# Copying a node table in interleaved 4 KB runs, and pacing GpSimd's gathers by small memsets

## What is computed

```python
deg = segment_sum(ones, row, num_segments=n)              # row = src, col = dst
deg_inv = where(deg > 0, rsqrt(maximum(deg, 1.0)), 0.0)
norm = deg_inv[row] * deg_inv[col]
h_j = h[col]                                              # h = relu(layernorm(x))
c_e = comps[edge_type]
msg = einsum('ebd,bdf->ef', c_e[:, :, None] * h_j[:, None, :], bases)
msg = msg * alpha[edge_type] * norm[:, None]
out = x + segment_sum(msg, row, num_segments=n)
```

## Time and profile before

| | us |
|---|---|
| median of 3 runs | 745.38 (742.51 to 745.63) |
| the profiled execution | 752.15 |
| its span | 750.2 |
| busy: DVE / PE / POOL / ACT | 596.4 / 574.7 / 540.3 / 370.1 |
| GpSimd's first scatter starts | 212.62 |
| its last scatter starts | 742.16 |

### The profile page before, as it was taken

How to read it: one execution, slowest core, us unless ns; L and a number is a source line. 1 busy time by engine, 2 the same in 40 slices (tenths; PEclk the granted TensorE clock), 3 DMA queues, 4 the chain that set the end, 5 groups by cost and what they waited for, 6 DMA issues and landing times.

```text
span 750.2 us, 13642 instructions
## 1 busy us (share of the span) xinstructions
PE 574.7 (77%) x3922; PEld 406.0 (54%) x3922; DVE 596.4 (80%) x2624; ACT 370.1 (49%) x1494; POOL 540.3 (72%) x404
## 2 busy tenths in 40 slices
PE   4999985665676876987778788886797878888860
PEld 4666654443454645655556565655565656665430
DVE  7999995466775676886987899986998999998730
ACT  0345542244424678664545655645656534446530
POOL 3788886455555587778788888878878767767775
PEclk9999998687788899999998999999999999999995
DMA  8999999989833335444535455444455545544332
GB/s 272 287 326 339 331 361 323 319 296 327 307 101 81 70 54 122 79 92 69 109 52 100 92 86 95 96 81 95 82 95 96 92 78 78 86 57 82 35 36 25
DMA packets 56574, 108.89 MB, mean 145 GB/s; under 512 B 9339, under 2 KB 48264, under 8 KB 55684
## 3 DMA queue, kind: packets, MB, share of 16 engines
q0 software_dynamic: 34496, 25.72, 25.6%
q1 hardware_dynamic: 4416, 50.68, 18.7%
q10 hardware_dynamic: 17588, 31.62, 13.5%
HBM read 94.89 MB, written 64.61 MB: 213 GB/s over the span
## 4 chain that ended last, share of the span: by engine, by line
DVE 14%; DMA 13%; issue 10%; PE 9%; POOL 8%; ACT 7%; ACTq 0%; POOLq 0%
DMA out_dram<-acc,scatter_idx 11%; POOL out_dram L393 6%; DVE masked L481 4%; DVE part_sum L518 4%; PE pst L756 3%; PE pst L737 3%; DVE turned_hot L475 2%; POOL rows L372 2%; DVE same L537 2%; ACT acc L651 2%; DMA rows<-in_x_dram,dst_i 2%; DVE rows L518 2%; ACT scratch L603 2%; PE pst L764 1%; ACT scratch L595 1%
## 5 line engine op out<-in xcount | busy, mean ns | idle before, releaser
L393 POOL DMA_INDIRECT out_dram<-acc,scatter_idx x196 | 313.8, 1601 | 106.3 <-issue 53.7
L372 POOL DMA_INDIRECT rows<-in_x_dram,dst_i x196 | 224.4, 1145 | 96.4 <-issue 36.2
L737 PE MATMUL pst<-table_bits,turned_hot 128*128 128x198 f16 x1568 | 183.1, 267 | 84.0 <-DVE masked L481 61.1
L756 PE MATMUL pst<-bases_sb,h_turned 128*128 128x512 f32 x392 | 214.1, 629 | 0.0
L737 PEld LDWEIGHTS pst<-table_bits,turned_hot 128*128 128x128 f16 x1568 | 147.3, 105 | 113.6 <-issue 59.1
L518 DVE SCALAR_TENSOR_TENSOR part_sum<-pst,coef,part_sum 128x128 f32<-128x128 f32 x392 | 115.7, 343 | 96.2 <-ACT part_sum L641 89.3
L764 PEld LDWEIGHTS pst<-rows,same 128*128 128x128 f32 x392 | 73.0, 199 | 166.2 <-issue 152.1
L641 ACT ACTIVATE part_sum<-pst,coef 128x128 f32<-128x128 f32 x196 | 71.2, 363 | 183.4 <-PE pst L756 132.3
L481 DVE SCALAR_TENSOR_TENSOR masked<-iota_h,lo,pst 128x198 f32<-128x198 f16 x392 | 141.9, 415 | 20.9 <-PE pst L737 16.3
L764 PE MATMUL pst<-rows,same 128*128 128x128 f32 x392 | 82.7, 294 | 58.4 <-ACT acc L651 57.4
L651 ACT ACTIVATE acc<-pst,sum_scale 128x128 f32<-128x128 f32 x196 | 71.5, 365 | 58.5 <-DMA out_dram<-acc,scatter_idx 28.9
(11 more groups left out here) (71 smaller groups left out, 415.8 us busy)
## 6 DMA issues: line engine op xcount, KB each, us to landing
out_dram<-in_x_dram SPq DMA_DIRECT2D x46, 1000.0 KB
src_row<-src_rows ACTq DMA_DIRECT2D x25, 512.0 KB
edge_row<-edge_rows ACTq DMA_DIRECT2D x45, 256.0 KB
out_dram<-in_x_dram ACTq DMA_DIRECT2D x4, 1000.0 KB
rows<-in_x_dram,dst_i POOLq DMA_INDIRECT x196
out_dram<-acc,scatter_idx POOLq DMA_INDIRECT x196
rows<-edge_rows ACTq DMA_DIRECT2D x10, 175.0 KB
edge_row<-edge_rows SPq DMA_DIRECT2D x4, 256.0 KB
```

Source lines behind the costliest of these rows:

```text
L372: pool.indirect_dma_start(row(t), None, x, bass.IndirectOffsetOnAxis(ap=dst_i[:, t:t + 1], axis=0)) \
L393: pool.indirect_dma_start(out, bass.IndirectOffsetOnAxis(ap=scatter_idx[:, t:t + 1], axis=0), acc[:, t % ACC_RING, :], None, compute_op=AL ...
L737: last = pe.matmul(pst[:, LOOK + t % 2, k * LO:(k + 1) * LO], turned_hot[:, g % 2, c, k * W + j * P:k * W + (j + 1) * P], table[:, c * LO: ...
L756: pe.matmul(pst[:, PRODUCT + t % 4, :], h_turned[:, g % 2, j, :], bases_sb[:].rearrange("d b f -> d (b f)"), start=True, stop=True).then_i ...
```

## The change

The first part replaces the copy's access pattern. Two consecutive transfers now share a block of 4,096 rows: one takes the even runs of 8 rows (4,096 bytes), the other the odd runs, 256 runs each. There are 48 such transfers of 1,048,576 bytes, and a 49th of the last 1,696 rows in the old form. The second part changes how gathers ahead of the copies' end are held back: 56 to 119 are each preceded by two memsets of a 128 by 40 tile, with a wait for the end of each, instead of waits on PE. `FIRST_GATHERS` rises from 108 to 120, and with it `gathers_until` and `stats_until`.

```diff
-    HIST_GATHERS = 56
-    LOOK_GATHERS = HIST_GATHERS + 4 * FIRST_LOOK * GROUP // 3
-    FIRST_GATHERS = LOOK_GATHERS + 3 * GROUP * SUM_STEP
+    HIST_GATHERS, FIRST_GATHERS = 56, 120
...
-    COPIES = 50
-    COPY_ROWS = N // COPIES
+    RUN_ROWS, RUNS = 8, 256
     COPY_RING = 2
+    PAIR_ROWS = 2 * RUNS * RUN_ROWS
+    COPIES = 2 * (N // PAIR_ROWS) + 1
+    LAST_COPY = (COPIES // 2) * PAIR_ROWS
...
+        beat = sb("beat", [P, 40])
...
-            a = i * COPY_ROWS
-            flat_out, flat_x = (y[a:a + COPY_ROWS, :].rearrange("r d -> (r d)") for y in (out, x))
-            engine.dma_start(flat_out.rearrange("(q e) -> q e", q=32), flat_x.rearrange("(q e) -> q e", q=32)) \
-                .then_inc(copied[i % COPY_RING], 16)
+            if i < COPIES - 1:
+                a = i // 2 * PAIR_ROWS
+                to, of = (y[a:a + PAIR_ROWS, :].rearrange("(q s r) d -> s q (r d)", s=2, r=RUN_ROWS)[i % 2]
+                          for y in (out, x))
+            else:
+                to, of = (y[LAST_COPY:N, :].rearrange("r d -> (r d)").rearrange("(q e) -> q e", q=32)
+                          for y in (out, x))
+            engine.dma_start(to, of).then_inc(copied[i % COPY_RING], 16)
...
-                elif HIST_GATHERS <= t < LOOK_GATHERS:
-                    pool.wait_ge(look_ps, (t - HIST_GATHERS) * FIRST_LOOK * GROUP // (LOOK_GATHERS - HIST_GATHERS) + 1)
-                elif LOOK_GATHERS <= t < FIRST_GATHERS:
-                    tile, part = divmod(t - LOOK_GATHERS, 3)
-                    if part == 0:
-                        pool.wait_ge(product_ready, tile + 1)
-                    else:
-                        pool.wait_ge(look_ps, FIRST_LOOK * GROUP + 2 * tile + part)
+                elif HIST_GATHERS <= t < FIRST_GATHERS:
+                    for _ in range(2):
+                        beats[0] += 1
+                        pool.memset(beat[:], 0.0).then_inc(beat_ended, 1)
+                        pool.wait_ge(beat_ended, beats[0])
```

More of the change, by code:

```diff
@@ L111, in sums_at @@
         return list(range(a + (b - a) * j // GROUP, a + (b - a) * (j + 1) // GROUP))
-    COPIES = 50
-    COPY_ROWS = N // COPIES
+    RUN_ROWS, RUNS = 8, 256
     COPY_RING = 2
+    PAIR_ROWS = 2 * RUNS * RUN_ROWS
+    COPIES = 2 * (N // PAIR_ROWS) + 1
+    LAST_COPY = (COPIES // 2) * PAIR_ROWS
     FIRST_COPIES = 4
-    assert COPIES * COPY_ROWS == N and COPIES % COPY_RING == 0
+    assert LAST_COPY < N and (N - LAST_COPY) * D % 32 == 0
     rows16_dram = nc.dram_tensor("edge_rows", (3, TILES * P), F16, kind="Internal").ap()
@@ L231, in build @@
         idx_ready = sem("idx_ready")
+        beat_ended = sem("beat_ended")
         type_row_loaded = [sem(f"type_row_loaded{b}") for b in range(TYPE_RING)]
@@ L301, in copy, with copies_done @@
                 engine.wait_ge(copied[i % COPY_RING], 16 * (i // COPY_RING))
-            a = i * COPY_ROWS
-            flat_out, flat_x = (y[a:a + COPY_ROWS, :].rearrange("r d -> (r d)") for y in (out, x))
-            engine.dma_start(flat_out.rearrange("(q e) -> q e", q=32), flat_x.rearrange("(q e) -> q e", q=32)) \
-                .then_inc(copied[i % COPY_RING], 16)
+            if i < COPIES - 1:
[6 more added lines that the diff above has]
+            engine.dma_start(to, of).then_inc(copied[i % COPY_RING], 16)
+        def copies_done(engine):
+            for b in range(COPY_RING):
+                engine.wait_ge(copied[b], 16 * len(range(b, COPIES, COPY_RING)))
         block = ctx.enter_context(nc.Block())
@@ L333, in _ @@
             sp.wait_ge(spare_filled, 16)
-            for b in range(COPY_RING):
-                sp.wait_ge(copied[b], 16 * (COPIES // COPY_RING))
+            copies_done(sp)
             for b in range(2):
@@ L351, in _ @@
                                pattern=[[1, P]], channel_multiplier=-1).then_inc(ident_ready, 1)
+            beats = [0]
             def pace(t):
@@ L381, in _ @@
             pool.wait_ge(spare_filled, 16)
-            for b in range(COPY_RING):
-                pool.wait_ge(copied[b], 16 * (COPIES // COPY_RING))
+            copies_done(pool)
             for t in range(TILES):
```

## The result

The changed kernel takes 772.75 us (median of 4 runs, 770.98 to 776.41), the kernel before 745.07 beside it (742.51 to 745.63). The ratio is 1.0385, with a 95% interval of 1.034 to 1.043. The forecast was 740 us, so it has the wrong sign. The profiled execution took 776.41 us with a span of 774.4; before it was 752.15 and 750.2. So 24.2 us have to be found in the two traces.

A forecast was written before the change was run, and what follows sets the result against it. GpSimd was taken to bound the kernel from 257 to 591 us. Terms -3.8 - 3.75 + 0 + 0 + 2 = -5.5 against the profiled 752.15 gave 746.6; with the median at 0.991 of profiled time, 740 us, range 728 to 757.

The forecast's parts named there:

- the price of a piece in part 2: DRAM copy: 4,096-byte pieces cost 175 to 215 ns, 0 to 31 us longer; 3 taken, end at 218 (215 to 246).
- 2.9 us for twelve gathers: Copy's end: the 12 added gathers cost 12 x 0.24 us of all sixteen DMA engines, so it ends 2.9 us later.
- rival A: Copy at the SBUF price: S, GpSimd's scatter start, at 246, 20 us late; +10, or 755 us; chance 0.21.
- Any S up to 226 is free: GpSimd's scatter start S: up to 226 us costs 0, because the eleventh scatter waits for `acc` until 254.63 anyway.
- given back as far as compute runs ahead: Behind the late scatter start: 8 of 19 idle us in 591 to 700 recovered, `acc` holding three tiles beyond today's lead.
- Part 1, the tail, -3.8: Main loop's end: twelve gathers moved ahead let 4.25 steps run at 10.64 instead of 11.54 us; -3.8, bounds 0 and -16.1.
- Part 2, the front, -3.75: Before the main loop: shorter copy pieces let an edge row load in time, removing DVE's 3.75 us wait; between 0 and 5.7.
- The Trainium skill's rule on packets: DMA queues: engines change queues only between packets, typically 9 to 17 descriptors; the front term would be 0 instead of -3.75.
- Part 3: Gathers ahead of the copy's end: two memsets make a 1.7 us cycle, the 64 gathers end at 217, ahead of 226; 0.
- wrong if the front changes by more than 6 us: Test set for the front: little there hangs on DMA but one wait, so a change above 6 us refutes the prediction.
- Rival C: Front gains 10 us rather than 3.75, as loads and instruction fetches no longer queue behind 64,000 bytes; -14, 731 us; chance 0.12.
- Part 4, +2: ACT's order: steps 8, 9 and 10 get one more 3.1 us statistics group each, partly hidden; +2, bounds 0 and 9.3.

The follow-up runs named there:

- e1: Kernel before with only the new copy (4,096-byte pieces, every second run), 108 gathers held back by the old waits: 773.6 us, ratio 1.0264 to the kernel before.
- e3: Changed kernel with its 4,096-byte pieces side by side, each transfer without gaps, the sixteen DMA engines on neighbouring pieces: 748.75 us, ratio 0.9939 to the kernel before.
- e12: Changed kernel with the old copy and six memsets instead of two ahead of each of 64 gathers, so that GpSimd starts late: 795.87 us (before 757.64).
- e2: Changed kernel with the old copy (64,000-byte pieces), keeping 120 gathers and the beat of two memsets: 748.56 us, ratio 0.994 to the kernel before.
- e17: Kernel before with the beat of two memsets alone, its own copy and 108 gathers: 742.8 us, ratio 0.9887 to the kernel before.
- e6: Changed kernel with interleaved copy runs of 32,768 bytes, every second one, instead of 4,096: 746.63 us, ratio 1.0047 to the kernel before.
- e8: Changed kernel with the old copy and 108 gathers instead of 120, beat kept: 743.79 us, ratio 1.0004 to the kernel before.
- e16: Kernel before with only the copy changed, to 8,192-byte runs side by side; own waits and 108 gathers: 751.42 us, ratio 0.9985 to the kernel before.
- e18: Changed kernel with 8,192-byte copy runs side by side and 108 gathers instead of 120, beat kept: 742.56 us, ratio 0.9874 to the kernel before.
- e11: Kernel before, unchanged, profiled once more: 750.31 us, where another single execution on the same chip took 757.64.
- e7: Changed kernel with the old copy, 120 gathers, and neither memsets nor waits ahead of the 57th to 120th: 748.7 us, ratio 1.0025 to the kernel before.

## Why the prediction was wrong, point by point

**The step that failed is the price of a piece in part 2.** The two ends, 175 and 215 ns for 4,096 bytes, were worked out, and then 3 of the 31 us between them were taken, because "a kilobyte is no dearer in small pieces" and the difference was put "down to the kind of transfer". The runs show 222 ns. Put into the same working: 12,288 x 47 / 16 = 36 us, 212.3 + 36 + 2.9 = 251.2; the copy ended at 250.9. So even the upper end, 246, was too low. That the sum meets the measured end to 0.3 us is in part luck: its 2.9 us for twelve gathers do not show, since e1 has 108 gathers and its first scatter comes at 252.42, no earlier. The reason was wrong in a second way. The prediction asked what the size of a piece costs, and on that it was nearly right: without gaps, e3 shows 184 ns and a start at 225.8. What it never asked is what the pattern of addresses costs. The 215 ns came from broadcast loads, which read one and the same run of DRAM for all 128 partitions, so that they stood near 222 is a coincidence, not a confirmation of rival A's reason.

**The free limit held.** "Any S up to 226 is free" gives 251 - 226 = 25 us; the eleventh scatter is 25.0 us late (279.65 against 254.63) and the thirteenth 24.95. e3, with its first scatter at 225.81, costs nothing.

**Rival A had the mechanism, at 755.** With S = 251 instead of 246 its own sum is 25 - 8 - 3.8 + 2 = +15, or 760 us. Another 12 are missing, 9 of them in the profiled execution. Its 8 us "given back as far as compute runs ahead" did not come, and e12 against the changed kernel shows the same: 19.4 us at the start are 19.6 at the end. The rows say where they went. Behind the last gather GpSimd did catch up, to 14.5 us late at tile 126, but the turned groups, which is compute, were then 24.1 us late and stayed so, with DVE busy for 55.08 of the 59 us from 591 to 650. So GpSimd had to wait for `acc` again, and the idle time in the earlier trace rows was no slack but the wait for that chain. That the ring of six `acc` is what had made compute as late as GpSimd is argued, not tested: 57.8 us of ACT's idle time ahead of the copies into `acc` are put down to scatters, 31.0 of them the one wait above.

**Part 1, the tail, -3.8: about -2, and not to be seen in time.** The four steps from the 31st to the 35th turned group took 38.7 us instead of 40.8, so the twelve gathers gave 2.1 us. GpSimd's lead at tile 126 was gone by tile 162, 23.6 us late again, and at the last scatter 1.3 us are left of what it had caught up since tile 108. The row of 10.2 us steps, given as the reason for a lower bound of 0, was the better guide than the mean of 11.54. Nor do the times show it: with the same old copy, 120 gathers had 0.994 (e2, before at 753.12) and 108 had 0.9887 (e17, before at 752.87), and on one chip 120 gathers took 746.63 us (e6, whose copy was no slower) and 108 took 743.79 (e8).

**Part 2, the front, -3.75.** In the trace it is there: from the first to the fifth turned group 65.8 us instead of 69.3, -3.5, and a load of an edge row lands in 10.3 us, with 2.2 us of DVE's idle left. In time it is not. e16, which has only that, is at 0.9985: its first to fifth turned group takes 66.9 us, but the first came later (141.18), so that the fifth is at 208.03, no earlier than before (205.84). And e18, whose fifth comes at 192.44 against 197.97 in e17, takes the same time as e17. The Trainium skill's rule on packets (DMA: Bandwidth & Descriptors, section "Queues, rings and completion order"), cited in the prediction, decides nothing here: SP's queue shows one packet for each 4,096-byte piece (4,938 for 19.00 MB, completions counted). The prediction left open how a copy in DRAM is packed, but the earlier trace rows has it: 777 packets for 24.64 MB are 385 pieces of 64,000 bytes and about as many completions, one packet a piece.

**The other front, which the prediction put at nothing.** Part 3 costed the beat (1.57 us in most cycles and 1.65 in the mean against 1.7, from 116.1 us on instead of 108.0, end at 221.4 against 217, both under 226) but never what the removed waits on PE's counters cost. The first turned group came 4.8 us earlier, and "wrong if the front changes by more than 6 us" came true: it is 8.3 us at the fifth. Rival C had the size but gave it to the DMA; e1, with the new copy and the old waits, has its fifth group at 207.5. In the changed kernel the copy hides all of it.

**Part 4, +2: nothing in the end, though larger on its way.** Two copies of turned groups on ACT (the 9th and the 13th) show it:

```profile
304.31 0.58 ACT L640 ACTIVATE h_turned<-pst 128x512 f32<-128x512 f32 x1
...
365.95 0.58 ACT L640 ACTIVATE h_turned<-pst 128x512 f32<-128x512 f32 x1
```

From the 9th to the 13th it takes 61.6 us, before 48.3 (283.39 to 331.73). By the 18th the lateness is back at 24.4. e2, which has the 120 gathers and their order of statistics, takes 61.4 us there, and e8, with 108, 48.2. So it comes with the order, and GpSimd hides it: its scatters stay 23 to 26 us late all through this stretch.

**Sum, as measured at GpSimd's scatters:** +24.95 us at the thirteenth, +0.65 from there to tile 108, -1.35 from there to the last: 24.25, against 24.2 in the spans.

## What to carry to other kernels

Price a DRAM-to-DRAM copy by its pattern of addresses as well as by the size of its pieces: here 4,096-byte pieces side by side were nearly free, the same pieces with gaps cost a fifth more on top, and one run of the pattern alone would have told it. When the unknown price of one edit sets when an engine that is already the bound may start, take the end of the range on which the engine's start depends seriously: past its free limit nearly every microsecond was paid here, and idle time further down was no credit against it, since another chain with little slack set it.

## What the runs showed of the hardware

- A copy in DRAM by runs of 4,096 bytes, every second one: 52.7 to 55.0 ns of a DMA engine for 1,000 bytes; side by side 45.0; runs of 8,192 bytes 43.8 with gaps and 42.1 to 43.6 without; runs of 32,768 and 64,000 bytes with gaps 41.8 and 41.6; flat pieces of 64,000 bytes 41.0 to 43.8 over seven traces. Gaps on the reading side alone 51.2, on the writing side alone 48.7. Whether the gap does it, or two transfers in flight that share a block, was not separated.
- A gapped copy with the engines, by its access pattern, 120 KB instead of 128 KB apart and 53 transfers instead of 49 was slower (start 269.06 instead of 251.21), not faster.
- Two memsets of 128 by 40 with a wait for each, and the gather's dispatch behind them, make a beat of 1.57 us, 0.34 + 0.27 + 0.96, in most cycles, and 1.65 in the mean of the changed kernel.
- While GpSimd waits on counters that PE raises, DVE showed idle of 2 to 8 us with releaser "remote" in the looks (e16, e11, e1, before), none without waits and beat (e7), and at most 0.8 with the beat. The trace doesn't name the cause.
- The kernel before has medians of 744 to 753 us depending on the chip, the kernel with the beat and 108 gathers 743 and 744 on one chip of each kind.
